# A two-layer graph network on one core: two PSUM banks for the second layer's dense sums, and the moves of a sum one step apart

## The reference

```python
deg_out = segment_sum(edge_weight, src); deg_in = segment_sum(edge_weight, dst)
norm = edge_weight * rsqrt(deg_out[src] * deg_in[dst] + EPS)
def layer(x, W, b): return relu(segment_sum((x @ W)[src] * norm[:, None], dst) + b)
gnn = layer(layer(xn, W6, b6), W7, b7) @ Wp + bp
x = x + gnn + mix(xn)          # linear attention over all nodes, 4 heads
x = x + ffn(_layernorm(x))     # 2 experts of 8 picked, gelu, layer norm
```

## Time and profile before

| | us |
|---|---|
| median of 3 runs | 3734.83 (3727.17 to 3735.6) |
| the profiled execution, its own time | 3725.99 |
| its span, first to last instruction | 3724.2 |
| first layer, its first `mm` to the second's first | 1533.6 |
| second layer, its first `mm` to its last | 1285.2 |

### The profile page before, as it was taken

How to read it: one execution, slowest core, us unless ns; L and a number is a source line. 1 busy time by engine, 2 the same in 40 slices (tenths; PEclk the granted TensorE clock), 3 DMA queues, 4 the chain that set the end, 5 groups by cost and what they waited for, 6 DMA issues and landing times.

```text
span 3724.2 us, 52328 instructions
## 1 busy us (share of the span) xinstructions
PE 2986.8 (80%) x16152; PEld 1996.9 (54%) x16152; DVE 1807.5 (49%) x4528; ACT 1147.4 (31%) x4063; POOL 2168.3 (58%) x2090
## 2 busy tenths in 40 slices
PE   4777837888888888878874688888888888888998
PEld 3445514555555555555542356555555555555666
DVE  9989835666666666656542133223222424222334
ACT  5777834443444444444330011001000101002211
POOL 4666656666666777666664666665666666630000
PEclk8899967998999999999996789889988989998999
DMA  4331134544545445445455535553555454533221
GB/s 118 98 102 57 56 78 132 173 140 137 173 138 163 150 139 173 135 142 167 129 194 177 124 126 168 192 187 106 193 193 191 148 192 149 190 101 106 78 77 47
DMA packets 219543, 515.58 MB, mean 138 GB/s; under 512 B 62465, under 2 KB 129831, under 8 KB 208169
## 3 DMA queue, kind: packets, MB, share of 16 engines
q0 software_dynamic: 88704, 243.35, 22.8%
q1 hardware_dynamic: 124053, 262.34, 20.7%
q10 hardware_dynamic: 6500, 6.40, 0.6%
HBM read 384.88 MB, written 127.07 MB: 137 GB/s over the span
## 4 chain that ended last, share of the span: by engine, by line
PE 33%; another core or an unknown queue 11%; issue 4%; DVE 3%; DMA 1%; ACT 1%; DVEq 0%; POOL 0%; SPq 0%; ACTq 0%; POOLq 0%
PE ps L698 13%; PE ps L867 5%; PE ps L880 4%; PE ps L659 3%; PE ps L676 3%; PE ps L818 1%; PE ps L815 1%; PE ps L803 1%; PE ps L708 0%; PE ps L638 0%; DVE wb L1274 0%; PE ps L827 0%; DVE accb L1244 0%; DVE ab L1297 0%
## 5 line engine op out<-in xcount | busy, mean ns | idle before, releaser
L1954 POOL DMA_INDIRECT ringb<-t,src x1848 | 1859.2, 1006 | 984.6 <-issue 494.6
L698 PE MATMUL ps<-xb,ab 125*128 125x256 f32 (+1 forms) x4700 | 1229.6, 402 | 87.3 <-issue 85.4
L698 PEld LDWEIGHTS ps<-xb,ab 125*128 125x128 f32 x4700 | 927.6, 201 | 355.1 <-issue 194.0
L676 PE MATMUL ps<-mlb 128*125 128x300 f32 x1260 | 476.9, 470 | 160.7 <-ACT side L1735 63.0
L1731 ACT ACTIVATE ab<-ps 125x250 f32 x724 | 294.7, 407 | 827.8 <-PE ps L676 410.7
L659 PE MATMUL ps<-ringb,Sb 128*32 128x257 f32 (+1 forms) x3696 | 358.7, 419 | 112.5 <-issue 46.3
L676 PEld LDWEIGHTS ps<-mlb 128*125 128x125 f32 x1260 | 224.6, 201 | 324.1 <-issue 281.6
L1927 POOL TENSOR_TENSOR ab<-ab,wn 128x100 f32<-128x100 f32 x201 | 274.1, 1369 | 169.5 <-DVE ab L1080 169.5
L600 PE MATMUL ps<-ab 128*50 128x125 f32 x3228 | 221.4, 284 | 135.6 <-ACT ab L1653 47.3
L1264 DVE TENSOR_TENSOR mlb<-iof,rel 128x900 f32<-128x900 f32 (+1 forms) x231 | 232.3, 1006 | 186.7 <-remote 129.9
L1653 ACT ACTIVATE ab<-ab,wn 128x50 f32<-128x50 f32 x1212 | 286.8, 328 | 21.1 <-DVE ab L1080 21.0
(11 more groups left out here) (245 smaller groups left out, 2704.3 us busy)
## 6 DMA issues: line engine op xcount, KB each, us to landing
ad<-ab SPq DMA_DIRECT2D x42, 1600.0 KB
ab<-ad SPq DMA_DIRECT2D x42, 1600.0 KB
ringb<-t,src POOLq DMA_INDIRECT x1848
kvd<-mlb SPq DMA_DIRECT2D x50, 256.0 KB, 2.1
kvb<-kvd SPq DMA_DIRECT2D x50, 256.0 KB
x2t<-mlb SPq DMA_DIRECT2D x13, 500.0 KB
xb<-x2t SPq DMA_DIRECT2D x13, 500.0 KB, 8.2
xb<-in_x SPq DMA_DIRECT2D x10, 625.0 KB
```

The lines of the kernel that those rows point to most:

```text
L676: e.matmul(PS[bank_of(t)][0:R, 0:HR], low[:, slot_of(t), :], high[:, slot_of(t), :], start=True, stop=True).then_inc(s_bld, 1)
L698: ins = e.matmul(PS[3][:, 0:wd], lhs, X[0:R, k, 0:wd], start=k == 0, stop=k == NT - 1)
L1954: e.indirect_dma_start(msg[:, slot * QT + k, 0:width], None, table, bass.IndirectOffsetOnAxis(src[:, t:t + 1], 0)).then_inc(s_g[slot], 16)
```

## The change

It changes tables and banks; no arithmetic is added or removed.

1. Second layer: chunks alternate between banks 3 and 7 (`dense_bank`). The first product of a chunk waits for the add of the chunk two before it, not one. The products of a chunk are spread over all 8 of its steps, 7, 6, 6, 6, 7, 6, 6, 6. The stream's three products share bank 6, with one wait added (L806 of the new file: the hidden product of a stage waits for the last copy of the stage before). The builds take banks 2, 4 and 5.
2. Both layers: lift, turn and add stand in three steps. A chunk's FIN is 2 steps later in the table and its lift stands in step FIN - 2, its turn in FIN - 1, its add in FIN. In both layers these are the first, second and third step after the one with the last product. A sparse group's lift and turn come one step earlier, its add stays.
3. First layer: the products begin one step later, 8 steps with 7, 6, 6, 6, 7, 6, 6, 6 and three without. The bank is still 3 alone.

```diff
-        MULT_AT[0].setdefault((_d + 1) * PD + 2 + _k * (PD - 2) // NT, []).append((_d, _k))
+        MULT_AT[0].setdefault((_d + 1) * PD + 3 + _k * (PD - 3) // NT, []).append((_d, _k))
-SPAN1 = NQS[1] - 2 - FROM1
+SPAN1 = NQS[1] - 3 - FROM1
-FIN_AT = [{(d + 2) * PD: d for d in range(ND)}, {}]
+FIN_AT = [{(d + 2) * PD + 2: d for d in range(ND)}, {}]
-        MULT_AT[1].setdefault(AT1[_c] + 1 + _k * (AT1[_c + 1] - AT1[_c] - 1) // NT, []).append((_c, _k))
-    FIN_AT[1][AT1[_c + 1]] = _c
+        MULT_AT[1].setdefault(AT1[_c] + _k * (AT1[_c + 1] - AT1[_c]) // NT, []).append((_c, _k))
+    FIN_AT[1][AT1[_c + 1] + 2] = _c
+FIN_AHEAD = [1, 1]
...
-            return (4, 5)[t % 2] if t >= tile_of(DY) else (2, 7, 5)[t % 3]
+            return (2, 4, 5)[t % 3] if t >= tile_of(DY) else (2, 7, 5)[t % 3]
+
+        def dense_bank(L, d):
+            return (3, 7)[d % 2] if L else 3
 
         def banks(t):
-            return 2 if t >= tile_of(DY) else 3
+            return 3
...
-                    if L == 1 and d >= 1:
-                        e.wait_ge(s_add, NU[0] + ADD_NO[1]["c", CH[1][d - 1]] + 1)
+                    if L == 1 and d >= 2:
+                        e.wait_ge(s_add, NU[0] + ADD_NO[1]["c", CH[1][d - 2]] + 1)
...
-                if s in FIN_AT[L]:
-                    dense_turn(L, FIN_AT[L][s])
+                if s + FIN_AHEAD[L] in FIN_AT[L]:
+                    dense_turn(L, FIN_AT[L][s + FIN_AHEAD[L]])
                 for d, k in m[:2]:
                     dense(L, d, k)
-                if s in ADD_AT[L]:
-                    turn(L, ADD_AT[L][s])
+                if s + 1 in ADD_AT[L]:
+                    turn(L, ADD_AT[L][s + 1])
...
-                B_hid, B_out, B_tr = (PS[b] for b in ((0, 1, 3) if j else (2, 6, 7)))
+                B_hid, B_out, B_tr = (PS[b] for b in ((0, 1, 3) if j else (6, 6, 6)))
...
+                    if m == 0 and ci >= 1:
+                        e.wait_ge(c_cp[j], 2 * ci)
...
-                    if s + 1 in ADD_AT[0]:
-                        lift(0, ADD_AT[0][s + 1])
+                    if s + 2 in ADD_AT[0]:
+                        lift(0, ADD_AT[0][s + 2])
...
-                    if s + 1 in FIN_AT[0]:
-                        lift_chunk(0, FIN_AT[0][s + 1])
+                    if s + 1 + FIN_AHEAD[0] in FIN_AT[0]:
+                        lift_chunk(0, FIN_AT[0][s + 1 + FIN_AHEAD[0]])
```

More of the change, by code:

```diff
@@ L697, in dense @@
                 lhs = A[d % 2 if L == 0 else (ND + d) % 2][:, k, :]
-                ins = e.matmul(PS[3][:, 0:wd], lhs, X[0:R, k, 0:wd], start=k == 0, stop=k == NT - 1)
+                ins = e.matmul(PS[dense_bank(L, d)][:, 0:wd], lhs, X[0:R, k, 0:wd], start=k == 0, stop=k == NT - 1)
                 if k % 10 == 9:
@@ L702, in dense_turn @@
             def dense_turn(L, d):
-                bank = PS[3]
+                bank = PS[dense_bank(L, d)]
                 e.wait_ge(s_lc, L * ND + d + 1)
@@ L1252, in add_chunk @@
                 o, n = (acc if L else acc3)[:, :, bass.ds(b, P)], 2 if L else 3
-                e.tensor_tensor(o, o, PS[3][:, 0:n * P].rearrange("p (h c) -> p h c", h=n), ALU.add).then_inc(s_add, 1)
+                e.tensor_tensor(o, o, PS[dense_bank(L, d)][:, 0:n * P].rearrange("p (h c) -> p h c", h=n), ALU.add).then_inc(s_add, 1)
                 added[0] += 1
@@ L1708, in lift_chunk @@
                     e.wait_ge(s_tc, L * ND + d)
-                e.activation(agd[:, 0:wd], PS[3][:, 0:wd], ACT.Copy).then_inc(s_lc, 1)
+                e.activation(agd[:, 0:wd], PS[dense_bank(L, d)][:, 0:wd], ACT.Copy).then_inc(s_lc, 1)
             tile_columns = TileColumns(e, "at")
@@ L1832, in stream @@
                 wd = n * R
-                B_hid, B_tr = (PS[0], PS[3]) if j else (PS[2], PS[7])
+                B_hid, B_tr = (PS[0], PS[3]) if j else (PS[6], PS[6])
                 if seg in ("relu0", "relu1"):
@@ L1858, in act_program @@
                 for s in range(STEPS1):
-                    if s + 1 in ADD_AT[1]:
-                        lift(1, ADD_AT[1][s + 1])
+                    if s + 2 in ADD_AT[1]:
+                        lift(1, ADD_AT[1][s + 2])
                     for t in BUILD_AT[1].get(s, ()):
@@ L1864, in act_program @@
                         stream(c, seg)
-                    if s + 1 in FIN_AT[1]:
-                        lift_chunk(1, FIN_AT[1][s + 1])
+                    if s + 1 + FIN_AHEAD[1] in FIN_AT[1]:
+                        lift_chunk(1, FIN_AT[1][s + 1 + FIN_AHEAD[1]])
                     clear1(s)
```

## The result

| | before | changed |
|---|---|---|
| median, us | 3733.0 (3727.17 to 3737.23) | 3720.33 (3709.24 to 3727.06) |
| the profiled execution's span | 3724.2 | 3718.5 |
| first layer | 1533.6 | 1535.1 |
| second layer | 1285.2 | 1282.0 |

The ratio is 0.9965, 95% interval 0.9955 to 0.9976: 12.7 us less, where 107 were forecast.

A forecast was written before the change was run, and what follows sets the result against it. PE was taken to bound both layers, POOL close behind. Second layer -70 - 26 - 4 and first layer -7 made -107 from 3725.99: 3619, stated as 3620 us, with 8 in 10 for 3545 to 3695.

The forecast's parts named there:

- PE bounds the second layer: Second layer: PE is the bound, POOL's gathers a floor some 15% below, its 217.5 us of slot waits due to PE.
- the feed's step: Second layer: four POOL gathers at 1.236 us each make a step of 4.94 to 5.01 us, against 5.95 taken.
- The work on PE stays: Both layers: PE's work is unchanged and only idle time changes; in the second layer the gaps at chunk ends go.
- Chunk ends, -70 and -26: Second layer: 20 chunks without builds gain 3.5 us each, -70; 5 with builds gain 5.2 us each, -26.
- The ordinary step: Second layer: a step, 5.60 us before, takes 5.29 with fewer products, 5.34 with the turn, if PE alone decided.
- First layer, -7: First layer: a third step without products costs 0.73 us a chunk, half the lift wait saves 1.06; -7 over 20 chunks.
- the rival that PE cools down: First layer: three steps without products lower PE's clock; 76.8 us a chunk against 66.95, 3823 us in all; chance 0.08.
- No change from the sparse groups, the stream, the build bank, the loads: Sparse groups in both layers nothing, 10 us either way; second layer's shared stream bank, third build bank and A loads nothing.
- The feed takes over: Second layer: PE waits at an empty ring instead of at chunk ends; chunks without builds 44 us, 3665 in all; chance 0.20.
- The gap is work: Second layer: PE still multiplies through the 8 us gap at a chunk's end; only -10, 3716 us; chance 0.09.
- the chunk of 39.33 us at clock 1.00: Second layer: one chunk before the change, PE 37.37 us busy, 27 gathers issued; taken as near the best, no room for backlog.
- -140 to -75: Whole kernel: the change in us of the prediction's own forecast case, range given as 3590 to 3655 us; chance 0.49.

The follow-up runs named there:

- the two edits of the stops: Changed kernel, POOL waiting for ring slots once per three steps: 4015.52 us of 3728.06, 1.0787; or allowed three steps ahead instead of six: 3777.93 of 3728.06, 1.0134.

## Why the prediction was wrong

**The step that failed** is the first one: that PE bounds the second layer and POOL "waits 129.6 + 87.9 = 217.5 us for ring slots, which PE frees". At the high level PE had finished; its report had not arrived, and reports come late only while POOL's gathers run. Leaving out 24 of 50 products gives 13 to 15 us, leaving out the gathers 330. I read POOL's two idle terms as slack that a quicker PE would take away, and they are part of what the feed costs, 213 us after the change. With them the feed's step is not 4.94 to 5.01 us but an estimated 4 x 1.47 = 5.88, against the 5.95 that a step took. At the low level there are no such waits, and the gathers' 1.24 to 1.27 us bound the layer by themselves.

A second step fell with it, in both layers: "The work on PE stays", so that only idle time changes. PE's idle time in the second layer did fall, by 35 us, and its busy time for the same work rose by 32; without gathers that work took 927 us instead of 1086.

- *Chunk ends, -70 and -26.* The turn's wait went as forecast (53.5 to 1.6 us), the time did not: 910.97 to 911.97 for 20 chunks without builds, 292.03 to 286.30 for the five with. The wait that was removed belonged to an engine that does not bound the layer.
- *The next thing late.* The ordinary step, forecast at 5.34 us, took 726.50 / 126 = 5.77: the silences that had fallen on chunk ends now fall on `mm` and products.
- *First layer, -7.* Nothing (1533.6 and 1535.1; alone, at the low level, 0.9999). The lift's wait did go (PE at L710 waited 6.1 us for ACT, 35.2 before), and the wait for ACT's copies of the builds grew (75.7 us, 63.0 before, and 94.3 and 61.2 more before builds that the profile puts down to nothing). Three steps without products and the eight others took 320.95 + 1018.99 us over 20 chunks, against 281.46 + 1057.53 for two and nine: the same to a microsecond. Idle time did what the sum said, 0.28 us a chunk less where it had 0.33, and the busy time for the same work took it back (0.33 a chunk more). The clock of the layer is 0.89 where it was 0.91, so the rival that PE cools down did not come in any size that counts.
- *No change from the sparse groups, the stream, the build bank, the loads*: right as far as the sum can show.
- *The rivals.* "The feed takes over" named the right engine and came too late: it had taken over before the change, so its time of 3665 was wrong too. "The gap is work" gave 3716, nearest to the result, and its sign, delays in the middle of chunks, is what the profile after shows. But its reason is refuted: the reports of the gap came together, within 0.12 us, not one by one as work would end, and leaving out 24 of 50 products made the layer only 11 to 19 us shorter. So its nearness is luck.
- *Against it I held* the chunk of 39.33 us at clock 1.00. It issued a gather each 39.33 / 27 = 1.46 us, the feed's usual pace; it was short because it used up what lay in the ring, and that can't be repeated.
- *Two slips that change nothing*: 4.94 to 5.01 us is 16 to 17% below 5.95, not 15, and -140 to -75 from 3726 is 3586 to 3651, not 3590 to 3655.

**What stays open.** What sets the level is not known: the same kernels met both, and so did one chip. The high level goes together with reports that the trace lacks; whether the writing of the trace takes part in it, and whether an execution without a trace has two levels, no run here shows. That reports are held while gathers run is shown by the second layer without gathers, where every one is on time; that a stop of POOL lets them through is argued from the table of stops, and the two edits of the stops bear it out in part only (64 stops in the second layer instead of 95 made it 72 us longer; the other edit made reports earlier but added two stops in that layer). Whether POOL's writing of the gathers or their traffic holds them was not separated. Whether PE itself is stopped by unsent reports (its single products with 0.4 to 1.0 us of "issue" between them in the stretch above suggest it) is argued, not shown.

## What to carry to other kernels

Before a wait is removed, don't take an engine's waits for its slack because another engine is named as the releaser. Ask of every wait whether the releaser's record ended just before it; if it ended several us earlier, the wait is not for that engine's work, and a second buffer won't shorten it. The cheapest test of a bound is to leave out half of the work of the engine that seems to bound: it would have told here, before any table was rewritten, that 24 of 50 products are worth 13 to 15 us.

## What the runs showed of the hardware

- The kernel before took 3369 to 3370 us or 3698 to 3733, each for a whole set of runs. The time up to the first layer (498 to 502 us) and that after the second (398 to 404) is the same in both; only the two layers, which have the gathers, differ.
- At the high level PE's reports come 0.8 to 1.5 us behind its records in the median while gathers run, and one in ten 5 to 8 us or more (changed kernel and kernel before), in bursts 0.04 to 0.1 us apart. Those reports of ACT and DVE that the trace has come within 0.01 us in the median; it lacks 36 to 42% of them there, and 2% at most at the low level. POOL's stops there take 1.33 us behind 4 gathers and 2.53 behind 12 (median, kernel before); at the low level the second layer has none over 0.6 us.
- PE busy time is no measure of its need: the same work took 1085.8 us in the changed kernel's second layer and 927.2 without gathers, at granted clocks of 0.90 and 0.98.
